# Graph attention and routed experts on one core: joined preparation, edge pass with PSUM operands, routing in batches, eight expert row buffers

## What is computed

```python
xn  = layernorm(x)                       # x: 6250 nodes x 256, 100000 edges sorted by dst
x_l = xn @ W_l + b_l ; x_r = xn @ W_r + b_r          # 8 heads of 32
g   = leaky_relu(x_r[dst] + x_l[src], 0.2)
a   = einsum('ehc,hc->eh', g, att) + log(edge_weight)
a   = softmax of a over the edges of each dst
x   = x + segment_sum(x_l[src] * a, dst) + bias
n   = layernorm(x)
top = the 2 best of 8 experts by n @ Wg + bg
x   = x + sum over top of (gelu(n @ W1[e] + b1[e]) @ W2[e] + b2[e])   # hidden 512
```

## Time and profile before

| | us |
|---|---|
| median of 3 runs (2311.33 to 2319.22) | 2318.75 |
| the profiled execution, its own time | 2322.45 |
| its span, first to last instruction | 2320.7 |
| schedule | 7.9 to 119 |
| project | 119 to 229.0 |
| edges | 229.0 to 1597.6 |
| route | 1597.6 to 1764.3 |
| experts | 1764.3 to 2259.3 |
| combine | 2259.3 to 2320.7 |

### The profile page before, as it was taken

One profiled execution on the slowest core, in us unless ns is written; L12 is line 12 of the kernel. 1 busy time (PEld: TensorE's weight loads), 2 busy tenths in 40 slices (PEclk: granted clock), 3 DMA queues, 4 the chain that ended last, 5 costly groups with the idle time before them and its releaser, 6 DMA issues. The chain is left out here.

```text
span 2320.7 us, 41397 instructions
## 1 busy us (share of the span) xinstructions
PE 1857.6 (80%) x9613; PEld 1475.1 (64%) x9614; DVE 1551.7 (67%) x2927; ACT 1039.7 (45%) x2678; POOL 1433.8 (62%) x1370
## 2 busy tenths in 40 slices
PE   0198589999899999998999989983667888888860
PEld 0077366677677776766777767762656777777750
DVE  2866578788788887988878888888655333333324
ACT  0111256676676666766666667663211222222210
POOL 0466777777777777777777777754225444444430
PEclk9999799999999999999999999997568999999985
DMA  4266566666666665666566656642901111111119
GB/s 149 52 218 242 147 195 178 181 190 188 184 183 180 188 188 177 191 181 185 179 182 184 188 173 191 185 132 84 288 0 46 59 59 57 59 57 59 59 51 321
DMA packets 203472, 348.65 MB, mean 150 GB/s; under 512 B 42984, under 2 KB 101616, under 8 KB 203136
## 3 DMA queue, kind: packets, MB, share of 16 engines
q0 software_dynamic: 53760, 150.08, 23.7%
q1 hardware_dynamic: 128616, 176.70, 22.9%
q10 hardware_dynamic: 20936, 20.41, 2.6%
HBM read 292.55 MB, written 55.72 MB: 150 GB/s over the span
## 5 line engine op out<-in xcount | busy, mean ns | idle before, releaser
L710 POOL DMA_INDIRECT rows<-left_rows,idx x896 | 1039.9, 1161 | 279.7 <-issue 266.7
L1013 PE MATMUL p_row<-rights,hotT 128*128 128x256 f32 x1792 | 527.2, 376 | 60.1 <-issue 42.2
L1015 PE MATMUL p_row<-rows,ident 128*128 128x256 f32 x1792 | 546.2, 387 | 0.0
L1075 PE MATMUL p_gain<-W,hots 128*128 128x264 f32 x1792 | 509.5, 409 | 9.3 <-ACT W L984 5.6
L933 ACT ACTIVATE L<-p_row 128x512 f32<-128x512 f32 x448 | 267.8, 598 | 440.4 <-PE p_row L1015 402.1
L1013 PEld LDWEIGHTS p_row<-rights,hotT 128*128 128x128 f32 x1792 | 337.9, 195 | 139.7 <-issue 63.9
L1075 PEld LDWEIGHTS p_gain<-W,hots 128*128 128x128 f32 x1792 | 328.3, 194 | 107.4 <-issue 50.9
L780 DVE TENSOR_TENSOR L<-L,attb 128x1024 f32<-128x1024 f32 x224 | 272.1, 1215 | 63.2 <-issue 33.7
L973 ACT ACTIVATE far<-iota_row,dl 128x128 f32<-128x128 f32 x896 | 304.7, 391 | 0.0
L898 DVE TENSOR_TENSOR acc<-acc,p_gain 128x264 f32 x448 | 189.4, 423 | 170.7 <-PE p_gain L1075 149.8
L1015 PEld LDWEIGHTS p_row<-rows,ident 128*128 128x128 f32 x1792 | 282.0, 194 | 0.0
(11 more groups left out here) (248 smaller groups left out, 1792.2 us busy)
## 6 DMA issues: line engine op xcount, KB each, us to landing
rights<-right_rows SPq DMA_DIRECT2D x448, 256.0 KB, 3.0
rows<-left_rows,idx POOLq DMA_INDIRECT x896, 3.2
right_rows<-p_parts SPq DMA_DIRECT2D x50, 256.0 KB, 2.0
c_rows<-results SPq DMA_DIRECT2D x12, 1024.0 KB, 14.4
w<-in_L_ffn_W SPq DMA_DIRECT2D x16, 512.0 KB, 6.2
left_rows<-p_y SPq DMA_DIRECT2D x50, 132.0 KB, 1.8
kept_rows<-X ACTq DMA_DIRECT2D x50, 128.0 KB, 1.9
X<-kept_rows SPq DMA_DIRECT2D x50, 128.0 KB, 2.2
```

The source lines that it names most:

```text
L710: nc.gpsimd.indirect_dma_start(out=rows[:, g.slot(RINGS), n, :], out_offset=None, in_=d["left"][:, :], in_offset=bass.IndirectOffsetOnAxis ...
L1013: nc.tensor.matmul(to, hotT[:, g.slot(2), i, :], rights[:, g.slot(2), n, part * D:(part + 1) * D], start=(part == 0), stop=False)
L1015: last = nc.tensor.matmul(to, s["ident"][:, :], rows[:, g.slot(RINGS), i, 0:D], start=False, stop=True)
L1075: last = nc.tensor.matmul(p_gain[:, n, 0:D + H], hots[:, g.slot(2), i, :], W[:, g.slot(2), i, :], start=(m == 0), stop=(m == PAIR - 1))
```

## The change

- **Preparation.** `schedule` and `project` become one block, `prepare`. X comes in three pieces (7, 21 and 21 tiles) from SP's queue, the block ends are read straight from the input, and the statistics are taken in batches of 7 tiles. PE's loop over 49 tiles starts when the second piece's first statistics are there; the schedule's instructions are written into DVE's, POOL's, ACT's and SP's loops at fixed tiles. ACT norms (Identity with scale and bias) and copies the left side; the left bias is left out of the tile and put into the right bias and the output bias. The low part is taken on DVE for tiles 9 to 20. `kept_rows` leave from SP in batches of 7 tiles, the last two after the loop.
- **Key reads.** The strided reads of the item keys, which `edges` did at its start, are made in `prepare`.
- **Edge pass, operands.** The attention vector is copied once into PSUM, and `scale` reads it from there. ACT writes the exponential of the scores twice, to SBUF for the denominators and to PSUM (`p_weights`), and `weigh` reads PSUM.
- **Edge pass, one-hot of the sums.** The places come by a transfer that repeats them on all 128 partitions (256 KB for every 2 groups), and ACT makes the one-hot from them with two instructions; PE's spreading matmul is gone.
- **Edge pass, chunk.** Two scans instead of four. Two more rows of marks per item (same key as the first, as the last edge of the pair) are prepared, spread by PE and copied by ACT, and two scalar_tensor_tensor instructions raise the maxima. The one-hot of the fall and its scaling go from DVE to ACT; one matmul is added. Stage offsets are further apart (`WEIGH, SUM = 11, 14`), and `L` has 4 buffers instead of 2.
- **Edge pass, length.** 220 groups (`LIVE`) are worked on instead of 224, with fewer stages for the rest. The denominators lie beside each head (33 columns), so that one instruction rescales.
- **Route.** 49 tiles, in 7 batches of 7: divide, add, moments, norm, transposes and gate overlap; ACT norms; the choice is made in 3 parts (21, 21, 7 tiles); 5 small instructions between count and map are gone. The residual and weight loads are issued first, the stores of the normed rows last.
- **Experts.** 8 row buffers; 7 loads ahead of the first send, and load(t + 7) is issued before send(t); PE's loop is unrolled by 8.

The diff, cut to its core:

```diff
@@ edges, VectorE
 def scale(g):
     wait(v, rectified, 2 * g.n + 2)
-    own = L[:, g.slot(2), :, :, 0:C].rearrange("p n h c -> p n h c")
-    nc.vector.tensor_tensor(own, own, attb[:, :].rearrange("p (h c) -> p h c", c=C).unsqueeze(1)
+    own = L[:, g.slot(APART), :, :, 0:C].rearrange("p n h c -> p n h c")
+    clear_of = 1 if TURN - 1 <= g.c % (2 * TURN) < 2 * TURN - 1 else 0
+    nc.vector.tensor_tensor(own, own, p_weights[:, clear_of, SPAN:SPAN + D].rearrange("p (h c) -> p h c", c=C).unsqueeze(1)
                             .to_broadcast([P, G, H, C]), ALU.mult).then_inc(scaled, 1)
 def weigh(g):
...
     rows[:, g.slot(RINGS), :, 0:D].rearrange("p n (h c) -> p n h c", c=C),
-    weights[:, parity(g), at:at + G, :].unsqueeze(3).to_broadcast([P, G, H, C]),
+    p_weights[:, parity(g), at * H:(at + G) * H].rearrange("p (n h) -> p n h", h=H)
+    .unsqueeze(3).to_broadcast([P, G, H, C]),
     ALU.mult).then_inc(weighed, 1)
 def raise_first(g):
...
+    nc.vector.scalar_tensor_tensor(K[:, :], M[:, 0, :], carry[:, 0:1], F[:, 1, :],
+                                   ALU.add, ALU.max).then_inc(peaked, 1)
@@ edges, ScalarE
+def part(g):
+    wait(act, locals_in[g.slot(4) // 2], (g.turn(4) + 1) * 16)
+    wait(act, hot, g.n)
+    nc.scalar.activation(apart[:, :], locals_[:, g.slot(4), :], ACT.Abs, bias=s["iota_column"][:, 0:1],
+                         scale=-1.0).then_inc(parted, 1)
@@ edges, SyncE
 def load_locals(g):
+    if g.c % 2 == 0:
+        r = g.slot(4)
+        wait(sp, parted, g.n - 2)
+        sp.dma_start(locals_[:, r:r + 2, :].rearrange("p a e -> p (a e)"),
+                     flat_locals[bass.ds(g.n * (G * P), 2 * G * P)].partition_broadcast(P)
+                     ).then_inc(locals_in[r // 2], 16)
-pipeline(sp, GROUPS, [(1, load_rights), (TURN, load_locals), (0, load_chunk)], 2 * TURN)
+pipeline(sp, GROUPS, [(1, live(load_rights)), (4, live(load_locals)), (6, load_chunk)], 2 * TURN, TURN)
@@ edges, TensorE
-pipeline(pe, GROUPS, [(0, sum_rows(0)), (1, spread_locals), (-SUM, gain(0)), (-4, turn_back),
-                      (-4, let_fall), (0, sum_rows(1)), (-2, spread_ends), (-SUM, gain(1)),
-                      (-1, turn)], 2 * TURN)
+pipeline(pe, GROUPS, [(0, live(sum_rows(0))), (-2, turn), (-5, let_fall), (-SUM, live(gain(0))),
+                      (-3, spread_ends), (-4, turn_back), (0, live(sum_rows(1))), (-SUM, live(gain(1))),
+                      (0, spread_mark(0)), (0, spread_mark(1)), (0, spread_mark(2))], 2 * TURN, TURN)
@@ experts, GpSimd
-for t in range(4):
+for t in range(LEAD):
     load(t)
 for t in range(SLOT_TILES):
+    if t + LEAD < SLOT_TILES:
+        load(t + LEAD)
     send(t)
-    if t + 4 < SLOT_TILES:
-        load(t + 4)
@@ prepare, GpSimd
+                    if t >= 0 and t not in on_vector:
+                        pool.wait_ge(right_steps, 2 * t + 2)
...
+                    if t == 8:
+                        pool.wait_ge(items_done, 1)
+                        pool.wait_ge(padded, 16 * 6)
+                        for q in range(QI):
...
+                    if t == 26:
+                        pool.wait_ge(local_done, 1)
@@ prepare, VectorE
+                for t in range(NODE_TILES):
...
+                    take_right(t)
+                    take_high(t)
+                    if t in on_vector:
+                        take_low(t)
+                    b = (t + 6) // BY
+                    if (t + 6) % BY == 0 and 2 <= b < BATCHES:
+                        take_stats(b)
...
+                    if 2 <= t < 2 + QI:
+                        find(t - 2)
...
+                    if t == 22:
+                        v.wait_ge(gathered[0], 16 * QI)
```

More of the change, by code:

```diff
@@ L113, in pipeline @@
     first = max(1, -(least // un))
-    turns = max(first, (steps - max(most, 0)) // un)
+    turns = max(first, (steps - max(most, unrolled)) // un)
     for c in range(-most, first * un):
@@ new lines, in multiply @@
+                def multiply(t):
+                    pe.wait_ge(x_turned_copied, t + 1)
+                    wait(pe, left_done, t - 1)
+                    wait(pe, right_steps, 2 * (t - 1) - 1)
+                    for side, wide in enumerate((DL, D)):
+                        for h in range(KD):
+                            last = nc.tensor.matmul(py[:, t % 2, side, 0:wide], xT[:, t % 2, h * P:(h + 1) * P],
+                                                    W[:, h, side, 0:wide], start=(h == 0), stop=(h == KD - 1))
+                    last.then_inc(projected, 1)
@@ new lines, in root, with norm @@
+                def root(b):
+                    act.wait_ge(sqrt_ready, b + 1)
+                    nc.scalar.activation(std[:, 1, tiles_of(b)], std[:, 0, tiles_of(b)], ACT.Sqrt).then_inc(sqrt_done, 1)
+                def norm(t):
+                    act.wait_ge(scaled, t // BY + 1)
+                    wait(act, x_turned, t - 1)
+                    nc.scalar.activation(xn[:, t % 2, :], X[:, t, :], ACT.Identity, bias=shift[:, t:t + 1],
+                                         scale=std[:, 2, t:t + 1]).then_inc(normed, 1)
@@ L940, in one_hot @@
                     wait(act, summed, 2 * g.n - 2)
[L941 to L944 removed]
+                    nc.scalar.activation(hotT[:, g.slot(2), :, :].rearrange("p n e -> p (n e)"), apart[:, :],
+                                         ACT.Relu, bias=unit[:, 0:1], scale=-1.0).then_inc(hot, 1)
@@ new lines, in _ @@
+                invert(0)
+                for t in range(RT + 1):
+                    if t % BY == 0 and t + BY < RT:
+                        invert(t // BY + 1)
+                    if t < RT:
+                        add(t)
+                    if t >= 1:
+                        take_stats(t - 1)
+                    if t % BY == 0 and t >= BY:
+                        take_moments(t // BY - 1)
+                    if t % BY == 2 and t >= BY:
+                        scale(t // BY - 1)
+                scale(BATCHES - 1)
@@ L1342, in _ @@
-                last.then_inc(counted, 1)
+                for t in range(RT + 2):
+                    if t < RT:
+                        turn(t)
+                    if t >= 2:
+                        gate(t - 2)
+                pe.wait_ge(consts, 9)
+                for n, (a, z) in enumerate(PARTS):
+                    pe.wait_ge(masked, n + 1)
+                    for i, m in enumerate((before, every)):
+                        last = nc.tensor.matmul(pc[:, i, a * EXPERTS:z * EXPERTS], m[:, :], both[:, a:z, :].rearrange("p t e -> p (t e)"),
+                                                start=True, stop=True)
+                    last.then_inc(counted, 1)
```

1234 lines of the change are left out of this document (654 added, 580 removed).

## The result

The changed kernel takes 1969.62 us (median of 4 runs, 1968.79 to 1970.93), the kernel before 2318.82 beside it: a ratio of 0.850, with a 95% interval of 0.848 to 0.852. The prediction was 1977 us. The profiled execution has a span of 1967.8 us against 2320.7, so 352.9 us have to be found. The timeline gives the ends of the stages.

The account below looks back on a forecast made before the run. It took POOL's gathers, delayed by DVE, to bound the edge pass, TensorE second. Terms -65 - 4 - 155 - 47 - 71 = -342 gave span 1979, execution 1981, forecast 1977 us; range 1920 to 2070.

Parts of the forecast that it names:

- a start inside such an instruction costs what is left of it: Edge pass: gathers wait for DVE instructions with two SBUF inputs; freed, they take 0.95 + 0.30, 5.00 us a group.
- Rival A: Edge pass: the two PSUM operands don't free the gathers, 220 x 5.85, total 2109 us; chance 6%.
- GpSimd's 5.05 and 0.20 for coupling: Edge pass, per group: POOL at 5.05 us as the largest of four engines, plus 0.20 for coupling, 5.25.
- Rival B: Edge pass: ACT or PE, loaded to 95% and more, set 5.6 us a group, +77, total 2054; chance 15%.
- 220 x 5.25: Edge pass: 220 groups at 5.25 us, 1155 against 1310, -155 us; bounds -199 and -23.
- The end of the pass: Fill-up at the end of the edge pass: two more gain-only groups, fewer sums at its start; 0, bounds -8 and +8.
- Preparation -56.9 for -65: Preparation: loop starts at 31 us, takes 121, last kept rows add 12, block end 164 instead of 229.0; -65 us.
- Route -38.0 for -47: Route: first batch ready after about 10 us, gate 58, choice -6, count and places -4; -47 us, bounds -35 and -62.
- Experts -81 for -71: Experts: 3.81 us a tile instead of 4.50, with 0.1 for loop ends; -71 us, bounds -50 and -82.
- Key reads: Start of the edge pass: PE's start moves from 15 to 11 us behind the barrier; -4 us, bounds 0 and -6.
- Rival D: Edge pass: landing of the places on SP's queue delays right tiles; slower, deciding from 6.8 us a group; chance 2%.
- Rival C: Everything overlaps as hoped: 5.07 us a group, preparation 155, gate at full clock, total 1920; chance 16%.

Follow-up runs that it names:

- e1: Changed kernel with the small operands of both products (attention vector and weights) read from SBUF again: 2102.5 us.
- e3: Changed kernel with only the weights read from SBUF again: 2021.0 us; the run between, with only the attention vector from SBUF: 2032.7 us.
- e7: Changed kernel with the batches of kept rows stored sooner in the preparation, one instead of two after the loop: 1968.4 us.
- e5: Changed kernel with four row buffers in the experts and tile t sent ahead of loading tile t + 4: 2053.0 us.
- e4: Changed kernel with ScalarE's loop of the edge pass unrolled over 32 groups instead of 16: 1976.3 us.
- the filler: Changed kernel with one more bf16 multiplication of 512 columns per tile on TensorE in the routing, its result unread: 2002.4 us.
- e9: Changed kernel with ScalarE's and VectorE's edge-pass loops unrolled over 32 groups: 2427.2 us, while the kernel before took 2581.

## Why the prediction was right, and where it wasn't

- **Gathers.** The reading "a start inside such an instruction costs what is left of it" is shown by e1 to e3, less 0.13 us a time: 957 ns against the foretold 970, and 127.5 of the 176 us. That a PSUM operand costs VectorE nothing is measured now (1.21 us for 1.22); the 0.56 at worst rested on no row. Rival A is out.
- **The bound of the new pass.** This step named the wrong engine. It took GpSimd's 5.05 and 0.20 for coupling. The run with three gathers keeps 5.19, so it isn't GpSimd. By the rows it is TensorE's own work (foretold 4.97, measured 4.94) and its 0.25 of waits, two thirds of them at the loop ends. Rival B had this mechanism, at 5.6; its size was wrong. GpSimd's 5.0 lay close under it, so the size came out nearly right. But by my step a cheaper gather would have been worth more, and a quarter of them left out gives 8 us.
- **Groups: 220 x 5.13** for 220 x 5.25. Four groups fewer are 23 of the 176 us; with e1's 127.5 that leaves some 26 for the two sweeps, the one-hots moved to ScalarE and the wider offsets together. Their single shares weren't tried.
- **The end of the pass** was put at 0 within 8 and is +7.6: the step said that it starts with fewer sums, and it starts with more. TensorE's gains, before in 1549 to 1598 us, then after in 1311 to 1366:

```profile
L1075 PE MATMUL p_gain<-W,hots 128*128 128x264 f32 x108 | 30.6, 427 | 9.3 <-ACT W L984 5.6 <-DVE W L865 3.6
L1191 PE MATMUL p_gain<-W,hots 128*128 128x264 f32 x129 | 36.2, 415 | 9.1 <-DVE acc L983 8.6 <-ACT W L1099 0.2 <-issue 0.2
```

With 129 gains for 108, and 32 sums for 22, TensorE is busy for 44.0 us instead of 35.5; the gains wait for the same 9. No run varies the offsets.

- **Preparation -56.9 for -65.** From 31 us on, as foretold, the loop takes 131 us for 121. That it starts as foretold is luck in part: two of the 49 tiles are multiplied ahead of it, from 19.9 us on, which the sum didn't have. PE is busy for 106.3 us: 47 tiles at 2.09 are 98, the 21 turns of places, sources and weights, which the sum left out, are 5.7, and the rest, by my estimate, is half clock behind pauses (a granted clock of 0.50 from 101 to 106 us, behind the 5.5 us in which PE stands for tile 23). It is idle for 25, where the lateness was put at 19. At tile 23 (91.4 to 100.5 us) three bursts of VectorE meet: 2.4 of statistics, 0.8 and 4.7 of places. Near tiles 16 and 17 the left copies wait 3 us each for the store of four tiles before to land, which wasn't in the sum. The tail was 10 for 12, and e7 shows its cause.
- **Route -38.0 for -47.** The first norm stands 15.3 us into the block, not 10. The step left out the landing of the first kept rows (5.2 us). The gate then takes 61.3 for 58, at half clock (0.50) as foretold. Choice and count are -9 for -10.
- **Experts -81 for -71.** 3.72 a tile is the floor of 3.71; the 0.1 for loop ends isn't seen. e5 gives the cause.
- **Key reads** -5.2 for -4. Rival D is out: TensorE waits 1.6 us in all for right tiles. Rival C asked for a gate at full clock and a preparation of 155, neither of which came.

## What to carry to other kernels

When an indirect gather beside VectorE is now and then long, lay the starts of the long ones over VectorE's instructions: if they end a fixed time after one with two SBUF inputs, move one input to PSUM before anything else. Then find out whether that engine is still the bound by leaving a quarter of its work out, not from busy shares: four engines within a tenth of each other look alike in a profile, and more work taken off the freed one may pay nothing. Where every engine's loop ends at the same group, making one engine's ends rarer may gain nothing, as in e4.

## What the hardware showed that I had not expected

- A gather that starts inside a scan or a scalar_tensor_tensor with two SBUF inputs is held as by a tensor_tensor, to 0.82 us after the end of the raises and 0.75 to 0.76 after that of the scan. The scan with one input in PSUM doesn't do it: the six gathers that start inside L887 take 0.95. A long copy with its only input in SBUF does, and it also holds gathers that started ahead of it.
- TensorE ran the gate for 57 us at 99% busy and a granted clock of 0.50, and for more than 80 us with the filler; in the mapping that begins 12 us behind it, the granted clock is 1.00 in the windows from 1464 us on. What tells these apart wasn't found.
- A kernel can take 11% more at another time (the kernel before 2581 us), though its packets take hardly longer: the queue of the gathers was busy for 541 us in e9 and for 523 in the changed kernel.
